# Attention stage: the residual load moved three transposes forward on SP, the residual addition moved behind the first context product on VectorE

## The reference

```python
x = x + _L0_attn_a_ref(_layernorm(x), W, b)           # one row's value, broadcast over the batch
x = x + _L0_ffn_ref(_layernorm(x), W_r, W_k, W_v, mu_r, mu_k)
x = x + _L0_attn_b_ref(_layernorm(x), Wq, bq, Wk, bk, Wv, bv, Wo, bo)
x = x + _L0_ffn_ref(_layernorm(x), W_r, W_k, W_v, mu_r, mu_k)
```

## Time and profile before

| what | value |
|---|---|
| median of 3 runs | 1691.24 us (1684.25 to 1695.86) |
| the profiled execution's own time | 1688.51 us |
| its span, first to last instruction | 1686.7 us |
| PE / DVE / ACT / POOL busy share of the span | 89% / 88% / 78% / 58% |
| mean granted TensorE clock | 0.978 |
| attention stage, about | 300 to 1500 us of the span |

### The profile page before, as it was taken

The page is one execution under the profiler, slowest core; times in us unless marked ns, Lnnn a source line. Parts: engine busy times, 40 slices in busy tenths (PEclk is TensorE's granted clock), DMA queues, the critical chain, the costliest instruction groups (busy, mean ns, idle before and its releaser), DMA issues.

```text
span 1686.7 us, 46716 instructions
## 1 busy us (share of the span) xinstructions
PE 1507.2 (89%) x16866; PEld 1137.9 (67%) x16866; DVE 1477.0 (88%) x4009; ACT 1316.4 (78%) x2410; POOL 971.7 (58%) x791
## 2 busy tenths in 40 slices
PE   4999978898989899999999899999998999759998
PEld 3888745566666666666666666666666666548887
DVE  5999589898999899999998999999998999946885
ACT  4999667777878787878787878878787878747996
POOL 4565356665666566656665666666665656523443
PEclk7999999999999999999999999999999999979999
DMA  5233247889899999899998999899989889961332
GB/s 203 88 119 103 76 87 143 156 159 176 146 180 161 172 165 178 167 161 179 168 178 146 172 164 183 142 185 167 176 159 172 161 157 162 180 135 63 101 112 77
DMA packets 737916, 252.11 MB, mean 149 GB/s; under 512 B 703764, under 2 KB 722456, under 8 KB 737688
## 3 DMA queue, kind: packets, MB, share of 16 engines
q1 hardware_dynamic: 736168, 247.93, 76.1%
q10 hardware_dynamic: 1520, 1.18, 0.2%
HBM read 47.73 MB, written 25.17 MB: 43 GB/s over the span
## 4 chain that ended last, share of the span: by engine, by line
PE 52%; DVE 18%; DMA 11%; issue 8%; POOL 5%; SPq 4%; ACT 3%; POOLq 0%; ACTq 0%; DVEq 0%
PE banks L1480 11%; PE banks L1581 8%; DMA at_pt<-at_halves 7%; DVE at_prob L1168 7%; PE banks L659 6%; PE banks L1555 5%; PE banks L627 5%; PE banks L641 5%; DVE at_halves L1179 4%; DMA pre_raw<-at_c_halves 3%; PE banks L1497 3%; PE banks L1539 3%; SPq L968 2%; PE banks L1541 2%; PE banks L1540 2%
## 5 line engine op out<-in xcount | busy, mean ns | idle before, releaser
L1345 ACT ACTIVATE at_prob<-at_prob,at_top 128x256 f32<-128x256 f32 x1024 | 435.8, 497 | 103.7 <-DVE at_top L1168 98.4
L1168 DVE CUSTOM_DVE_ANT_0 at_prob<-banks,at_masks,pre_s_scale 128x256 f32<-128x256 f32 x1024 | 428.6, 478 | 15.1 <-PE banks L1581 0.7
L1179 DVE TENSOR_TENSOR at_halves<-at_prob,at_halves 128x1024 f16<-128x1024 f32 x256 | 314.2, 1243 | 0.9 <-ACT at_halves L1355 0.9
L1581 PE MATMUL banks<-at_kt,at_qt 32*128 32x256 f32 x4096 | 261.2, 391 | 52.8 <-DVE at_top L1168 26.0
L1480 PE MATMUL banks<-at_xt,pre_w_h 128*128 128x512 f16 x1024 | 297.8, 383 | 2.9 <-DVE at_v_l L1241 2.5
L1110 POOL TENSOR_TENSOR at_c_halves<-at_ctx,at_c_halves 128x1024 f16<-128x1024 f32 x64 | 136.6, 2134 | 274.9 <-DVE at_halves L1179 268.2
L1581 PEld LDWEIGHTS banks<-at_kt,at_qt 32*128 32x128 f32 x4096 | 209.3, 187 | 114.5 <-issue 111.9
L1539 PE MATMUL banks<-at_v_h,at_pt 128*128 128x65 f16 x2048 | 215.1, 195 | 67.3 <-DMA at_pt<-at_halves 35.0
L1355 ACT ACTIVATE at_halves<-at_prob 128x1024 f16<-128x1024 f32 x256 | 269.5, 1053 | 6.1
L1539 PEld LDWEIGHTS banks<-at_v_h,at_pt 128*128 128x128 f16 x2048 | 187.4, 98 | 125.3 <-issue 64.8
L1079 POOL TENSOR_TENSOR at_kt<-at_k_by 128x512 f32<-128x512 f32 x128 | 163.1, 1274 | 108.5 <-DVE at_halves L1179 108.4
(11 more groups left out here) (130 smaller groups left out, 3179.8 us busy)
## 6 DMA issues: line engine op xcount, KB each, us to landing
f_x<-in_x SPq DMA_DIRECT2D x16, 512.0 KB, 3.6
x_after_ffn<-f_x SPq DMA_DIRECT2D x16, 512.0 KB, 2.6
at_x_ln<-x_after_ffn SPq DMA_DIRECT2D x16, 512.0 KB, 4.6
at_x_res<-x_after_ffn SPq DMA_DIRECT2D x64, 128.0 KB, 3.0
x_after_attention<-at_x_res SPq DMA_DIRECT2D x64, 128.0 KB, 2.9
f_x<-x_after_attention SPq DMA_DIRECT2D x16, 512.0 KB, 4.3
out_x<-f_x SPq DMA_DIRECT2D x16, 512.0 KB, 3.0
at_tables<-in_cos SPq DMA_DIRECT2D x16, 256.0 KB, 3.7
```

What stands on the lines that cost most here:

```text
L1168: last = nc.vector.tensor_tensor_reduce(out=prob[:, n % 2, h, :], in0=s_ps[:, h, n % 2 * 2 * P:(n % 2 + 1) * 2 * P], in1=masks[:, kind, :] ...
L1179: nc.vector.tensor_tensor(halves[:, n % HB, 1, :, :], prob[:, n % 2, :, :], halves[:, n % HB, 0, :, :], ALU.subtract).then_inc(p_low, 1)
L1345: last = nc.scalar.activation(prob[:, n % 2, h, :], prob[:, n % 2, h, :], ACT.Exp, bias=top[:, n % 2, h:h + 1], scale=-1.0)
L1581: last = nc.tensor.matmul(s_ps[:, h, d * 2 * P:(d + 1) * 2 * P].rearrange("p (s t) -> p s t", s=2), qt[rows_of, par, half, b * P:(b + 1) * ...
```

## The change

Two lines move. On SP, `load_residual` leaves its place between p0 and the store, and stands at the end of the step: the block of step t's addition is loaded at the end of step t-1. On DVE, `residual` moves from the place in front of `v_low_of(t+1, 0)` and `context(t, 0)` to the place behind them. Nothing is added or removed; PE, ACT and GpSimd keep their order.

```diff
@@ sync, at_step(t)
             turn_p(t - 1, 3)
             turn_context(t - 2)
             turn_p(t, 0)
-            load_residual(t - 5)
             store(t - 6)
             if g == 0 and S >= 0:
                 load_tables(S + 1)
...
                 turn_x(S + 1)
             if g == 3:
                 load_x(S + 3)
+            load_residual(t - 4)
@@ vector, at_step(t)
             v_low_of(t + 1, 1)
             if g == 3 and S > -2:
                 shift_of(S + 2)
-            residual(t - 5)
             v_low_of(t + 1, 0)
             context(t, 0)
+            residual(t - 5)
             key_product(t + 2, 1)
             key_product(t + 2, 2)
```

## The result

The changed kernel takes 1723.12 us (median of 4 runs, 1717.15 to 1726.16) against 1691.72 us (4 runs) for the kernel before on the same chip: a ratio of 1.0196, interval 1.0167 to 1.0224. That is slower by 2.0%, about 33 us by the ratio (the two medians are 31.4 us apart). The forecast was 1702 us with a range to 1718: the sign was right, the size was not, and the time lies outside the range. The profiled execution took 1717.15 us, the shortest of the four, with this span.

A forecast was written before the change was run, and what follows sets the result against it. The prediction took the loop from DVE's p2 remainder through SP's transposes to PE's keys as the bound. 13.8 us of delays less 1.8 us saved made 12 us longer; it gave 1702 us, range 1678 to 1718.

The forecast's parts named there:

- The load on SP: SP's queue: the load behind p2 delays p3, the context transpose and p0 by 0.55 us each; p1 is unchanged.
- 25 places x 0.55 us = 13.8 us: PE's waits for transposes: 14 for contexts, ten for p0, one for p3, each longer by the load's 0.55 us.
- outer bound of 1.57 us: SP's load issue: upper limit of the delay per place, the longest issue of this load in the trace.
- not counted: PE's present slack in front of p0: left out of the sum; some lost where under 0.5 us, left to the range.
- The addition on DVE: DVE: the moved addition runs while PE makes the keys, so the key product starts when it did in step 16.
- The cover that I named: PE's key projection hides the moved addition; without it the addition costs at most 0.48 us a step, 30 us over 63.
- the 1.8 us that I counted: DVE: saving in four steps whose key product had no wait on PE, 0.45 us each.
- 1 us less in total: SP's shared DMA ring: using the ring-order rule alone, 0.53 us replaces 0.55 and lowers the sum by this.
- Rival A: DVE's addition: its load waits were the cause; removing 26.8 us gives 1662 us, half of it 1675; chance 0.13.
- Rival B: SP's load costs about 1 us at 25 places and eats p0's slack elsewhere: 1716 us; chance 0.2.
- Rival C: SP's queue: later transposes issue more shortly and land when they did; time within 5 us of 1689; chance 0.15.
- The tail: Behind step 63: SP waits for the store to land, but the last context transpose waits 5.1 us for GpSimd anyway; nothing counted.

The follow-up runs named there:

- thin_load: The changed kernel with each residual load bringing 32 of 256 columns (16 KB, not 128 KB) and the addition only scaling the projection: 1711.35 us, 1.0126 against the kernel before.
- store_too: The changed kernel with the store also moved in front of p3, ahead of the load: 1758.66 us, 1.0414 against the kernel before.
- others_only: The changed kernel with the load in front of p3 only where no second step follows, at its old place for second steps: 1701.81 us, 1.008.
- load_before_p0: The changed kernel with the load placed between the context transpose and p0 instead of in front of p3: 1712.12 us, 1.0131 against the kernel before.
- pe_kept_busy: The changed kernel with PE repeating the projection's first small matmul 12 times before waiting for the contexts in second steps: 1709.8 us, 1.0132 against the kernel before.
- second_only: The changed kernel with the load in front of p3 only where a second step follows, at its old place otherwise: 1709.26 us, 1.0111 against the kernel before.
- dve_only: The kernel before with only the addition moved on DVE, the load at its old place: 1689.98 us, 1.001 against the kernel before.
- sp_only: The changed kernel with the addition back at its old place, so only the load moves on SP: 1718.77 us, 1.0182 against the kernel before.

## Why the prediction was right and wrong

**The load on SP: mechanism right, sum wrong.** The step that failed is "25 places x 0.55 us = 13.8 us": the price came out at the contexts, 14 of the 25 places, but places were missing from the count, and a term was missing from the sum.

- *The price.* I took 0.55 us between the distance from load to store of the earlier trace rows and a third of the extra landing time of the earlier trace rows. Where PE waited already for the contexts, it came out: 22.4 - 14.4 us in 13 waits is 0.62 us each. The argument for it, that the place behind p2 is nearer to the short issues, is wrong. On the way into third and fourth steps, where the load stands directly behind p2, it takes 1.0 us to issue (means 0.99 and 1.03), and the p3 behind it starts 1.97 us after its remainder where it started 0.87 and 0.97 us after. On the way into first and second steps, with another instruction in front of the load, p3 starts only 0.43 and 0.76 us later than before. thin_load shows that the dear issue doesn't come from the bytes, store_too that it doesn't come from the load but from the place. The trace of before did not show that place; the range's outer bound of 1.57 us held it.
- *The count.* I had set p0's slack in the other steps aside as "not counted". Before, p0 landed on average 0.55, 0.54, 0.82 and 1.44 us ahead of PE's product in the four kinds of step; after, 0.20, 1.10, 0.18 and 0.52. In the first, third and fourth steps most of it is used up, and PE's waits for p0 go from 15 to 24 times and from 13.9 to 25.3 us in steps 5 to 61. Eleven of the 24, 12.5 us, are in third and fourth steps, where before has two, 1.5 us. others_only measures that at 13.1 us and load_before_p0 shows the same kind of wait by itself. Of p3 I counted one wait; on PE's timeline the p3 of first steps, behind the x transpose and the load, went from 4 waits and 3.0 us to 11 and 10.0. It is consumed in the second step, just ahead of the contexts.
- *The missing term.* The prediction had nothing on the clock. In second steps PE now waits longer for the contexts, up to 3.28 us, and seven projections run at a granted clock of 0.52 to 0.68. The trace of before showed such projections twice, and I didn't read the windows there. By their length it is 7.5 us; pe_kept_busy puts it at about 11 us, with intervals that leave 4 to 18.

With these, the loss adds up: 13 us in the first, third and fourth steps (others_only) and 20 us in the second ones (second_only), of which the clock is between a third (7.5 us) and a half (second steps of 21.56 instead of 22.16 us in pe_kept_busy). On bytes alone, the Trainium skill's rule in "DMA: Bandwidth & Descriptors", section "Queues, rings and completion order", that descriptors are consumed in ring order, would have the loss go with the load's bytes; by thin_load about a third of it does. (The prediction's "1 us less in total" for it is a slip: 25 x 0.02 us is 0.5.)

**The addition on DVE: right.** dve_only is 1.001. The cover that I named is there: the addition runs while PE is late. It is PE's key projection, as I had said: the key product starts 0.09 us behind it in every step. The four steps without that wait that I had found before the change are the other four of the 57 (PE's keys ended 0.2 to 0.8 us ahead there); the 1.8 us that I counted for them can't be told from nothing. One detail was wrong: I expected the key product's waits to grow from 12.1 us by about what vanished. They come to 14.4 us (0.3 under PE's name, and gaps of 0.3 us at most under "issue" that end with PE's keys too); the rest stands in front of the context, where PE's product with the values, behind p0, is what comes last.

**Rival A (the load's waits were the cause): refuted.** The waits went as it said, and the time went up. The sign that I had named, key products that wait less than 12.1 us, seems to come out on its side by the line of PE alone (0.3 us), and does not with the gaps that end with PE's keys (14.4). I should have named the sum of DVE's waits as the sign: 56.2 us before, 73.6 after, and 56.7 with the addition alone, at the time of before. The rule from the Trainium skill, "DMA: Bandwidth & Descriptors", section "Rules for kernel authors", to issue early and wait late, is met to the letter by sp_only, at 1.82% more time: here the early issue stands in front of transposes that are needed sooner.

**Rival B (a dearer delay): half of it is what happened.** p0's slack is eaten, as it said; its price of about 1 us is met in third and fourth steps alone, and not at the contexts (0.62). By its sign, waits for blocks and contexts up by over 20 us, it holds over steps 5 to 61 (38.3 to 63.7 us) and misses over 400 to 1500 (44.7 to 61.2). That its 1716 us come near the 1723 measured (the profiled execution took 1717.15) is in part luck: 25 x 1 us was too much for the places it counted, and the p3 waits and the clock were not in it. **Rival C (nothing): refuted** by the waits on PE.

**The rest.** p1 did not change (6.6 and 6.5 us of waits). The context waits were forecast at 21 us and are 22.4. The tail costs nothing: from step 61's p2 remainder to the end 242.4 us passed before and 241.6 after. The forecast of step kinds (first and second longer by half a us, the others as before) was wrong: the second grew by 1.14 us, and all the others by 0.2 to 0.3.

What stays open: why the first plain transfer behind p2 takes about 1 us to issue, and the exact shares of issue, bytes and clock, which overlap and were read from one experiment each (the clock's from the trace as well).

## What to carry to other kernels

In a queue that issues back to back in front of a consumer with less than a microsecond of slack, an instruction that is moved ahead can cost its issue at the new place in every round in which the slack behind it runs out, however long before its own deadline it lands; look for a place where the queue idles (here in front of p2: 1.0003 instead of 1.0196). Slack that a forecast sets aside as uncounted is the first thing that a delay eats: take the mean slack of every consumer behind the moved instruction, and compare it with the price. And where PE waits grow to some microseconds, read the granted clock of the work behind them before the wait is priced at its length alone.

## What the runs showed of the hardware

- A plain load or store of 128 KB took about 1.0 us to issue when it came first behind p2's transpose (means of 0.99 and 1.03 us for the load after the change, 1.02 and 1.03 for the store in store_too), 0.72 to 0.84 us (means by kind of step) when it came first behind p0's, and mostly 0.43 us behind another plain transfer; 16 KB instead of 128 KB changed nothing in that (medians of 906 and 912 ns).
- A projection that takes 2.9 us took 4.2 to 5.4 us in those seven steps, at a granted clock of 0.52 to 0.68 over it, behind PE waits of 0.8 to 3.3 us for the contexts. Twelve small matmuls without use, put in front of that wait in every second step, held the clock at 1.00 and made the program about 11 us shorter (4 to 18).
